# Moving every second drive product of a selective scan to GpSimd, with its decay in PSUM and the orders written anew

## What is computed

```python
def step(h, inp):
    u_t, dt_t, B_t, C_t = inp
    dA = jnp.exp(dt_t[:, :, None] * A)
    h = dA * h + (dt_t * u_t)[:, :, None] * B_t[:, None, :]
    y = jnp.einsum('bds,bs->bd', h, C_t)
    return (h, y)
```

## Time and profile before

| | |
|---|---|
| median of 3 runs | 1865.23 us (1862.81 to 1865.96) |
| the profiled execution | 1865.98 us, its span 1864.2 us |
| busy TensorE / VectorE / ScalarE / GpSimd | 1635.7 / 1468.0 / 1099.5 / 750.1 us |
| DMA | 309.17 MB |
| opening pass, second pass | 149.0, 198.0 us |
| middle passes | 210.9, 205.0, 205.0, 205.4, 204.8 us |
| closing pass, what follows the last scan | 194.3, 240.0 us |

### The profile page before, as it was taken

How to read it: one execution, slowest core, us unless ns; L and a number is a source line. 1 busy time by engine, 2 the same in 40 slices (tenths; PEclk the granted TensorE clock), 3 DMA queues, 4 the chain that set the end, 5 groups by cost and what they waited for, 6 DMA issues and landing times. The chain is left out here.

```text
span 1864.2 us, 24264 instructions
## 1 busy us (share of the span) xinstructions
PE 1635.7 (88%) x8352; PEld 765.6 (41%) x8352; DVE 1468.0 (79%) x2032; ACT 1099.5 (59%) x1474; POOL 750.1 (40%) x601
## 2 busy tenths in 40 slices
...
GB/s 192 241 248 234 257 236 202 180 183 201 200 144 159 185 233 130 188 187 206 191 153 172 194 241 102 199 177 227 170 154 191 192 229 113 109 0 0 1 7 6
DMA packets 107886, 309.17 MB, mean 166 GB/s; under 512 B 15971, under 2 KB 32245, under 8 KB 107765
## 3 DMA queue, kind: packets, MB, share of 16 engines
...
## 5 line engine op out<-in xcount | busy, mean ns | idle before, releaser
L1531 POOL TENSOR_TENSOR sb_hc<-sb_hst,sb_crep 128x512 f32<-128x512 f32 x512 | 654.2, 1282 | 880.5 <-DVE sb_hst L1259 623.2
L1259 DVE TENSOR_TENSOR_SCAN sb_hst<-sb_ring,ps_in 128x512 f32<-128x512 f32 x512 | 620.1, 1211 | 20.9 <-ACT sb_ring L947 16.0
L947 ACT ACTIVATE sb_ring<-sb_ring,sb_A 128x512 f32<-128x512 f32 x512 | 345.8, 713 | 211.8 <-DMA sb_ring<-spread_dram 189.7
L1251 DVE TENSOR_TENSOR ps_in<-sb_ring,ps_brow 128x512 f32<-128x512 f32 x512 | 354.9, 693 | 30.6 <-DMA sb_ring<-spread_dram 18.3
L924 ACT ACT_TABLE_LOAD x230 | 295.1, 1283 | 13.6 <-DVE sb_xd L1310 3.2
L858 PE MATMUL ps_pair<-sb_mix,sb_ew 128*128 128x512 f32 x512 | 250.4, 623 | 6.6 <-DVE sb_g L1348 2.7
L637 PE MATMUL ps_y<-sb_hc,sb_const 128*32 128x512 f32 x1024 | 149.8, 659 | 64.3 <-POOL sb_hc L1531 54.7
L799 PE MATMUL ps_pair<-sb_g,sb_h 128*128 128x512 f32 x320 | 160.6, 625 | 21.9 <-ACT sb_mix L1105 15.4
L787 PE MATMUL ps_pair<-sb_h,sb_g 128*128 128x512 f32 (+3 forms) x512 | 164.4, 452 | 8.2 <-DVE sb_nmax L1400 4.3
L858 PEld LDWEIGHTS ps_pair<-sb_mix,sb_ew 128*128 128x128 f32 x512 | 94.1, 196 | 147.0 <-issue 103.1
L878 PEld LDWEIGHTS ps_pair<-sb_ew,sb_eh 128*128 128x128 f32 x1024 | 120.4, 192 | 21.3 <-issue 18.4
(11 more groups left out here) (208 smaller groups left out, 1890.7 us busy)
## 6 DMA issues: line engine op xcount, KB each, us to landing
sb_ring<-spread_dram SPq DMA_DIRECT2D x512, 512.0 KB, 6.0
spread_dram<-sb_dd ACTq DMA_DIRECT2D x32, 512.0 KB, 6.6
...
```

Source lines behind the costliest of these rows:

```text
L947: act.activation(ring[:, n % RING, 0, :], ring[:, n % RING, 0, :], ACT.Exp, scale=A[d][:, g:g + 1]).then_inc(sem["dA"], 1)
L1251: dve.tensor_tensor(ps_in[n % 2][:], ring[:, n % RING, 1, :], ps_brow[:], ALU.mult).then_inc(sem["dbu"], 1)
L1259: dve.tensor_tensor_scan(hst[:, HST_SLOT[n], :], ring[:, n % RING, 0, :], ps_in[n % 2][:], 0.0, ALU.mult, ALU.add).then_inc(sem["scan"], 1)
L1531: pool.tensor_tensor(hc[:, n % 6, :], hst[:, HST_SLOT[n], :], crep[n // NU][:], ALU.mult).then_inc(sem["hc"], 1)
```

## The change

Every second unit (odd n, BY_POOL) is made another way. GpSimd multiplies dt*u by B's rows in place in the ring slot (`drives`, a new stream m, semaphore dbp), reading B's rows from SBUF. ScalarE writes the decay of such a unit into `ps_in[n % 2]`, now the bank of all odd units, and so waits until the scan two units back is done. The scan of such a unit takes the decay from PSUM and the drive from the ring, the other way round than before. Since VectorE's stream has no drive for odd units, it reads drive n, scan n-1, scan n, drive n+2. B's rows get a second buffer, one for each direction. All order strings are new.

```diff
-    dA=64, dbu=64, scan=64, hc=64, yskip=4, gated=4, resid=2, sq=6, rstd=6, norm=6,
+    dA=64, dbu=64 - len([n for n in range(64) if n % 2 == 1]), dbp=len([n for n in range(64) if n % 2 == 1]), scan=64, hc=64, yskip=4, gated=4, resid=2, sq=6, rstd=6, norm=6,
...
+BY_POOL = [n for n in range(UNITS) if n % 2 == 1]
+POOLED = [sum(m < n for m in BY_POOL) for n in range(UNITS + 1)]
...
     POOL=(
-        "rrurxruuuxxuxruuxurruuuurruuurrxxrxuuxxruuxuuuuruuuuuuxurrrurruxruuxuuxxrrxurxruxruxruxxruxxrrxuururrrrrrruuxu"
+        "uxuxmurmurumrmuumrxuuurumxuuxmuurxmxuumrxruururrmumrrruxxmrurrummruurmrurxmuuuuxxrxmrurruxummumuxuuxuururmxmru"
...
-        brep = sb("brep", [P, T])
+        brep = [sb(f"brep{d}", [P, T]) for d in range(2)]
...
-                act.activation(ring[:, n % RING, 0, :], ring[:, n % RING, 0, :], ACT.Exp,
-                               scale=A[d][:, g:g + 1]).then_inc(sem["dA"], 1)
+                dA = ring[:, n % RING, 0, :]
+                if n in BY_POOL:
+                    act.wait_ge(sem["scan"], row("scan", n - 1))
+                    dA = ps_in[n % 2][:]
+                act.activation(dA, ring[:, n % RING, 0, :], ACT.Exp, scale=A[d][:, g:g + 1]).then_inc(sem["dA"], 1)
...
-                        act.wait_ge(sem["brow"], row("brow", d))
-                        act.dma_start(brep[:], cut[d, 0:S, :].unsqueeze(1).broadcast_to([S, CU, T])).then_inc(sem["brep"], 16)
+                        act.wait_ge(sem["brow"], row("brow", d + 1 - NH))
+                        act.wait_ge(sem["dbp"], row("dbp", POOLED[NU * (d + 1)] - PER["dbp"]))
+                        act.dma_start(brep[d][:], cut[d, 0:S, :].unsqueeze(1).broadcast_to([S, CU, T])).then_inc(sem["brep"], 16)
...
             def scan(row, n):
-                dve.wait_ge(sem["dbu"], row("dbu", n + 1))
+                if n in BY_POOL:
+                    dve.wait_ge(sem["dbp"], row("dbp", POOLED[n] + 1))
+                else:
+                    dve.wait_ge(sem["dbu"], row("dbu", n - POOLED[n] + 1))
                 dve.wait_ge(sem["dA"], row("dA", n + 1))
+                dA, dbu = ring[:, n % RING, 0, :], ps_in[n % 2][:]
+                if n in BY_POOL:
+                    dA, dbu = dbu, ring[:, n % RING, 1, :]
...
             def units(at, prev):
                 for n in range(UNITS):
-                    drive(at(0), n)
-                    yield
+                    if n not in BY_POOL:
+                        drive(at(0), n)
+                        yield
...
+            def drives(at):
+                row = at(0)
+                for n in BY_POOL:
+                    pool.wait_ge(sem["brep"], row("brep", 16 * (n // NU + 1)))
+                    pool.wait_ge(sem[f"ring{n % RING}"], row(f"ring{n % RING}", 16 * (n // RING + 1)))
+                    pool.tensor_tensor(ring[:, n % RING, 1, :], ring[:, n % RING, 1, :], brep[n // NU][:], ALU.mult
+                                       ).then_inc(sem["dbp"], 1)
+                    yield
```

More of the change, by code:

```diff
@@ L235 @@
     PE=(
-        "xxxxxxuxrxxruxrxhrurhxrhruhxxrrrruhxrrhhurhruxrrruhxruxxrxxhxrxhxurrxhxrrrrrxrrrrrrrrrrrhruhhruhrhurrrruhrrrrr"
-        "urru"),
+        "xxxuxrrhuhxxrhrrxurrxhurrhrrxrxrhxxurrhurrrhrxrurxxurrxhhrrurrrxxrrhhurrrrrxhuhxrrxurxrxhhuxxrruxrrrrrrrrrruhr"
+        "rxhu"),
     ACT=(
-        "uxxxxuuxxxuuxurruuxuruhruuxruhxxrrhuhuuxxxruurxruruuhuhruuruhurururuuururuuxurhxuuuhxxruhxuxrhururrhxruuuruhrx"
-        "ruururrrrrrrrrxxrrhhrhuurhururuuruxrrruuururruuhurru"),
+        "uxxxuuuxrruuhuhhxxruuruuruhxrrxxuuurhrruurrxuuhruxuxuurrhuuuuruhrrrxuururhuurxxurruxhuruxxuhurrhruuhuruxrruuhx"
@@ L241 @@
+        "rurxrruruxuuxxuhrxrrurxuurrurxuruhurrrrruuurruhruruh"),
     DVE=(
-        "uxxurxxxuuguuuxxuuuuuxuxuuruxururxuuxhururuuxuuuhuhuruuhuxuuurruuuurruuxuhuguuuuuuuuuhuuxuhuuuuuuruuuhuuuuuhrr"
-        "ruxguxuuurrrruhruuxxuxxuurrxhxuuruuxrurrururrrxrrruhrrurrurruhuuurxhhhuuuuurruuuhururguruuuuruuuuururuurruuuuu"
-        "uruurhuuru"),
+        "uuuxugxuxxruuurhuuxruhurhuuuuuxrruxuurhxuuurrrhurruuxxuuuuhxuurgxuururrhxuuurruruuuuuruuuurxruxuuruxurrururgrh"
+        "xuhhuruxurhuhurrxururruuuhhuuuxuruuxruuuxrururuxruxuxrgrxxhuruuhuuuuurruuuururrrurruhhur"),
@@ L256 @@
+        "uuhguhuuthuuuuuhuuuuhuuuuu"),
     POOL=(
-        "uuuuuuuuuuuuuuuuuuuuuuuuuuuuuuuuuuuuuuuuuuuuuuuuuuuuuuuuuuuuuuuu"))
+        "mumumuuumuuumuuumuuumumumumuuumuumuumumuuumuumuumumuuumuumuuuummuumuuummuuummuuuumumuuumuuuumuum"))
 def without(order, streams):
@@ L1245, in drive @@
                     dve.wait_ge(sem["brep"], row("brep", 16 * (n // NU + 1)))
-                    dve.wait_ge(sem["dbu"], row("dbu", n))
-                    dve.tensor_copy(ps_brow[:], brep[:]).then_inc(sem["brow"], 1)
+                    dve.wait_ge(sem["dbu"], row("dbu", n - POOLED[n]))
+                    dve.tensor_copy(ps_brow[:], brep[n // NU][:]).then_inc(sem["brow"], 1)
                     dve.wait_ge(sem["brow"], row("brow", n // NU + 1))
@@ L1254, in scan @@
             def scan(row, n):
[L1255 removed]
+                if n in BY_POOL:
+                    dve.wait_ge(sem["dbp"], row("dbp", POOLED[n] + 1))
+                else:
+                    dve.wait_ge(sem["dbu"], row("dbu", n - POOLED[n] + 1))
                 dve.wait_ge(sem["dA"], row("dA", n + 1))
+                dA, dbu = ring[:, n % RING, 0, :], ps_in[n % 2][:]
+                if n in BY_POOL:
+                    dA, dbu = dbu, ring[:, n % RING, 1, :]
                 before = [m for m in range(UNITS) if HST_SLOT[m] == HST_SLOT[n]]
                 dve.wait_ge(sem["hc"], row("hc", 1 + max([m for m in before if m < n] or [before[-1] - UNITS])))
[L1259 to L1260 removed]
+                dve.tensor_tensor_scan(hst[:, HST_SLOT[n], :], dA, dbu, 0.0, ALU.mult, ALU.add).then_inc(sem["scan"], 1)
             def gate(at, ahead, hf, prev):
```

21 lines of the change are left out of this document (9 added, 12 removed).

## The result

The changed kernel takes **1925.05 us** (median of 4 runs, 1921.10 to 1927.97) against 1865.60 for the kernel before on the same chip (1862.81 to 1868.03): ratio 1.0316, 95% interval 1.0293 to 1.0339. It is slower by 59.5 us; the forecast was 1902, 36 us slower, in a range of 1850 to 1945. The profiled execution took 1921.1 us (span 1919.3), the shortest of the four.

The account below looks back on a forecast made before the run. PE and DVE, both near their limit, were taken to bound each pass as a chain alternating between them. Opening -3, second -12, five middle passes +35, closing +12, last stretch +4 gave +36: 1902 us, range 1850 to 1945.

Parts of the forecast that it names:

- the second pass: Pass without expert work, 198.00 us before: 177 by its work, taken as 186 because of 64 loads; -12 us.
- (a): Middle pass, first transposes (x3) to end of product fo: PE work moves behind fo, 106.2 us falls to 93.6.
- (b): Middle pass, fo to the last gated down product (eo7) on DVE: DVE ends last, its relief spent; 67.3 us.
- (c): Middle pass, eo7's product to exponential round e1 (a step, not a run): layernorm tail fully exposed; 7.4 us.
- (d): Middle pass, exponential round e1 (not a run) to the rounds' end: two reductions and one dt product fewer; 34.0 us.
- (e): Middle pass, end of the rounds to next x3: chain of single steps, 9.1 us plus 0.8 for softplus and loads; 9.9.
- Costs set to nothing: POOL's 32 products a pass, decays written to PSUM and their scan waits, B's second buffer: all taken as hidden, 0 us.
- a sign against me: Forecast would be wrong if scans waited for POOL or ACT by more than 5 us a pass.
- 1: Rival: DVE's relief arrives in full, PE alone bounds, middle pass 196 us, total 1802; chance 0.15.
- 2: Rival: gains and losses cancel, middle passes 205 to 208 us, total 1848 to 1870; chance 0.17.
- 3: Rival: coupling of decays, POOL's products and scans adds; a pass 217 to 220 us, total 1930 to 1950; chance 0.13.
- 4: Rival: DVE instructions reading two SBUF tensors and POOL lock each other out; +3 us a pass, total 1920; chance 0.05.

Follow-up runs that it names:

- e2: Kernel before with the change's orders only, all 64 drives on DVE and all decays in the ring; 1978.75 us.
- e7: The change with the products of the 12 even units 30 to 52, between fo's residual and eo7, also left out; 1917.00 us.
- e1: Run: kernel before's orders with the change's POOL products and PSUM decays, decays behind what they must wait for; 2040.87 us. "Round e1" is an exponential round instead.
- e0: Not a run: the exponential round ahead of round e1 in a pass, whose start is a mark on PE's timeline.
- e9: The change with the experts' sum in its own tile, so the first exponential no longer waits for the final layernorm; 1916.06 us.
- e11: The change with half of every ring load left out from the second pass on; 1923.56 us.
- e6: Kernel before with the change's orders, odd units' products left out, all decays in the ring; 1918.94 us.
- e5: Kernel before with the odd units' products left out, its orders, decays and POOL as before; 1853.81 us.
- e3: The change with odd decays written in place in the ring, without their wait for the scan two units back; 1957.43 us.
- e4: Old orders in every stream, odd decays in place in the ring, POOL's products as in the change; 1938.99 us.
- e12: Kernel before with the experts' sum in its own tile and DVE's final layernorm step moved behind the third gate; 1853.55 us.

## Why the prediction was right, and where it was wrong

**Sign and place: right.** Five middle passes were to give +35 and gave +41.2, the closing pass +12 and +13.4, the last stretch +4 and +5.5, the opening -3 and -2.2. By the profile that is +55.7 in all, against +36; the second pass, below, has half of the difference.

**The pieces: right in size.** By the forecast's own marks: (a) 93.6 against 95.0; (b) 67.3 against 68.2; (c) 7.4 against 6.0; (d) 34.0 against 34.2; (e) 9.9 against 9.8. Sum 212.2 against 213.2, 1 us too little in each of five passes. Four of them were longer still, by 6.3 us together (the longest, 216.2, at a granted clock of 0.99), where the kernel before had one such pass too, 5.9 us longer than the others.

**Step (b), its reason: half right.** "DVE ends last, and each relief on DVE has been spent" holds against e2, where the drives come back and cost 7.4. It fails in e7: without 12 more the stretch keeps 68.1 us, since PE's 62.7 us of work and 5.4 us of waits fill it as well. I had counted PE's work there as some 60 and gave it no waits. That DVE's sum nevertheless gave the right length was luck: it happens to equal PE's work with its waits. The 11 scans that I counted there before are those up to round e1; up to e0 there are 9, against 24 now.

**Step (c): the size right, the weight wrong.** The tail behind eo7 stood open as described, but with it gone (e9) a pass is 0.4 us shorter, not 3 to 5. PE was to wait 3 to 4 us ahead of e1; it waits 0.80 there, and 1.21 ahead of e0.

**The second pass: wrong**, -12 forecast, -2.2 measured, the largest miss of the sum. The piece up to fo was taken as 72 us, which is PE's own work there (72.8); but it lasts 85, so some 12 us of waits were left out. The piece from fo to e0 was taken as 58 and lasts 60, the rest as 47 and lasts 52. That makes 197 where I had 177 for work; the 9 that I added for loads are refuted by e11. In the timeline most waits up to fo stand right behind squares and normalisations, where without experts nothing fills PE's order; which of them weigh most wasn't tried.

**Costs set to nothing: right in the change's own orders** (e6, 0 a middle pass, some 6 us in all, which the profiles put into the opening pass), and only there: e1 is 187 us slower than e5, which has the orders before and no such products, and in a middle pass about a third of that is the lower granted clock. DVE waited for POOL's product 7.7 us in a middle pass, more than the 5 us that I had called a sign against me; the scans concerned stood in the hidden layers and the rounds, where DVE had time.

**Rivals.** 1 (the relief arrives in full) is refuted by e5, more strongly than the forecast had it: it has nothing to arrive at. 2 (gains and losses cancel) did not come: no middle pass was under 213. 3 is not what happened in the change, but is what e1 is. 4 is real for scans (e3, e4), and the change avoids it.

Six kernels differ in these two things (where a step had to be put in or back, as e1 and e2 say); in us:

| odd products | orders before | orders of the change |
|---|---|---|
| on DVE | 1865.6 | 1978.8 (e2) |
| left out | 1853.8 (e5) | 1918.9 (e6) |
| on POOL, decays in PSUM | 2040.9 (e1) | 1925.1 (the change) |

So the loss is the orders': they cost 113 us with all drives on DVE and 65 with none of the odd ones. The relief pays part of that back only because the orders had first made DVE a bound, and the mechanism needs orders like these, since with those before it costs far more. Whether some other orders would serve it without the loss is open. What makes a middle pass longer is that PE, with nearly the same work (1.2 us more), is idle 6.9 us more. That moving a step takes away such a wait is shown for one (e12, in VectorE's order of the kernel before); for those of the change it is read from the timeline.
